# The head of a two-layer transformer kernel: pass 0's rows scaled in four copies and turned on TensorE instead of copied by DMA, and another slot table

## The reference, cut to what matters

```python
x = layernorm(x + attn0(x)); x = layernorm(x + ffn0(x))   # ffn0: int8 matmul, rounded activations
x = layernorm(x + attn1(x)); x = layernorm(x + ffn1(x))   # ffn1: silu(x Wg) * (x Wu), then Wd
# x: 4 x 1024 x 128, 16 heads of 8
def attn0(x):
    q, k, v = split(x @ qkv_w.T)                    # each 1024 x 128
    q, k = l2norm(q) / sqrt(8), l2norm(k) / sqrt(8) # norm over all 128 of a row, not per head
    return softmax(q_h @ k_h.T / temperature_h) @ v_h ... @ proj_w.T + proj_b
# attn1: per-head layernorm of q and k, rotary embedding, causal mask
```

## Time and profile before

| what | us |
|---|---|
| median of 3 runs | 812.29 (812.27 to 813.13) |
| the profiled execution | 812.69 |
| its span in the trace | 810.6 |
| PE busy | 791.2 |
| ACT busy | 767.8 |
| DVE busy | 528.8 |
| POOL busy | 174.3 |

### The profile page before, as it was taken

One profiled execution on the slowest core, in us unless ns is written; L12 is line 12 of the kernel. 1 busy time (PEld: TensorE's weight loads), 2 busy tenths in 40 slices (PEclk: granted clock), 3 DMA queues, 4 the chain that ended last, 5 costly groups with the idle time before them and its releaser, 6 DMA issues.

```text
span 810.6 us, 18434 instructions
## 1 busy us (share of the span) xinstructions
PE 791.2 (98%) x7467; PEld 295.0 (36%) x7469; DVE 528.8 (65%) x1422; ACT 767.8 (95%) x869; POOL 174.3 (22%) x370
## 2 busy tenths in 40 slices
PE   8999999999999999999999999999999999999996
...
PEclk9999999999999999999999999999999999999999
...
GB/s 148 256 230 216 122 79 81 155 41 181 144 35 156 266 40 44 179 156 80 92 208 27 128 106 43 91 128 44 91 131 51 68 131 54 27 190 110 2 28 15
DMA packets 48554, 88.71 MB, mean 109 GB/s; under 512 B 5201, under 2 KB 14545, under 8 KB 48465
## 3 DMA queue, kind: packets, MB, share of 16 engines
...
...
...
## 4 chain that ended last, share of the span: by engine, by line
PE 73%; ACT 13%; DVE 9%; issue 4%; POOL 1%; DMA 0%; ACTq 0%; DVEq 0%; POOLq 0%
PE ps L896 35%; PE ps L874 20%; ACT probs L717 13%; PE ps L763 8%; PE ps L752 3%; PE ps L849 2%; DVE th L1282 1%; DVE hT L1283 1%; PE ps L930 1%; PE ps L757 1%; DVE sums_t L1137 0%; POOL v_all L590 0%; PE ps L938 0%; PE ps L791 0%; DVE gate_sb L1279 0%
## 5 line engine op out<-in xcount | busy, mean ns | idle before, releaser
L717 ACT ACTIVATE probs<-ps 128x1024 f32<-128x1024 f32 x800 | 745.8, 1057 | 17.6 <-PE ps L874 13.8
L896 PE MATMUL ps<-probs,v_st 128*32 128x512 f32 (+3 forms) x3584 | 424.9, 556 | 3.1 <-issue 1.8
L874 PE MATMUL ps<-q_st,k_st 32*128 32x512 f32 (+3 forms) x1792 | 257.0, 458 | 3.2 <-ACT probs L717 2.3
L874 PEld LDWEIGHTS ps<-q_st,k_st 32*128 32x128 f32 x1792 | 119.4, 181 | 289.5 <-ACT probs L717 240.7
L627 POOL TENSOR_SCALAR_AFFINE_SELECT probs<-probs 128x256 f32<-128x256 f32 x256 | 103.8, 428 | 139.1 <-ACT probs L717 137.0
L896 PEld LDWEIGHTS ps<-probs,v_st 128*32 128x32 f32 x3584 | 80.1, 108 | 109.2 <-issue 80.3
L595 POOL COPY v_st<-v_all 128x256 f32<-128x256 f32 (+1 forms) x65 | 25.7, 405 | 342.1 <-PE ps L896 334.2
L1256 DVE COPY mid_qkv<-ps 128x384 f32<-128x384 f32 x32 | 17.8, 557 | 44.3 <-PE ps L763 43.8
L1137 DVE STREAM_TRANSPOSE sums_t<-ps 128x512 f32<-128x512 f32 x32 | 22.9, 717 | 26.6 <-PE ps L896 26.5
L1287 DVE TENSOR_TENSOR last_y<-ps,last_y 128x128 f32<-128x128 f32 x24 | 7.0, 292 | 42.7 <-PE ps L763 42.7
L849 PE MATMUL ps<-yTp,w_hid 128*128 128x512 f32 x84 | 30.8, 448 | 2.2 <-DVE hT L1283 0.6
(11 more groups left out here) (192 smaller groups left out, 645.2 us busy)
## 6 DMA issues: line engine op xcount, KB each, us to landing
...
q_st<-parts_scratch SPq DMA_DIRECT2D x62, 256.0 KB, 3.9
...
k_st<-parts_scratch SPq DMA_DIRECT2D x17, 256.0 KB, 2.8
xT<-in_xT SPq DMA_DIRECT2D x8, 256.0 KB, 4.4
x_all<-in_x SPq DMA_DIRECT2D x8, 256.0 KB, 6.5
out<-yo SPq DMA_DIRECT2D x7, 256.0 KB, 2.3
```

The lines of the kernel that those rows point to most:

```text
L717: nc.scalar.activation(probs[:, k % PS, :, 0:w], slot(k)[:, :, 0:w], ACT.Exp).then_inc(probs_ready, 1)
L874: last_ = mm(slot(k)[:, e, at:at + n], k_st[row, p % KB, kt * P:(kt + 1) * P], q_st[row, p % KB, lo:HALF], start=True, stop=not shifted)
L896: last_ = mm(acc[HR * h:HR * (h + 1), lo:HALF], v_st[:, p % VB, kt, h, :], probs[:, (2 * s + h // 2) % PS, h % 2, at:at + n], start=FIRST[ ...
```

## The change

The parts for pass 0 are no longer copied by DMA. DVE scales k and q of chunk 0 for the first four heads into `first_qk`, each feature four times side by side (y = 0 to 3); PE turns this, so the four copies come out on the right partitions; ACT writes the turned values times sign (1 or -1) rounded to fp32r, `first_sign`; and DVE writes turned x low + first_sign, with low 0 or 1, which is the high part for two of the copies and the negative low part for the others, to `k_st` and `q_st` in place. The second key half of pass 0 (chunk 1) is made in the same way as a new side piece, `firstT`, the first of FIRST_KEYS.

Other edits that go with it: chunk 0's projection is done as all q, all k, all v, in banks ACC, SIDE and 5; the squares of k come from DVE's batch-norm statistics, and of chunk 1 ACT takes two tiles' squares and DVE the others; the flags are worked out in two portions, the second behind the scaling; the plain scaling, turning and splitting of chunk 0 (for pass 1 and later passes) stands behind the work for pass 0, the turns behind score blocks 0 to 2; the copies for pass 1 are all issued by SP, the high part's ahead of the low part's; pass 1's second key half is copied straight from SBUF and no longer through DRAM; POOL stores chunk 1's k later in its list; SP issues the loads of later constants only when the first input is in; the zero matmuls are 8 at the start and no others. The slot table is another one throughout.

```diff
-FIRST_KEYS = [("prep", 1, "pe", "qkT", 1), ("prep", 1, "dve", "scale_q", 0), ("prep", 1, "pe", "qkT", 0)]
+FIRST_KEYS = [("prep", 1, "pe", "firstT", 1), ("prep", 1, "dve", "scale_k", 0), ("prep", 1, "pe", "qkT", 1), ("prep", 1, "dve", "scale_q", 0), ("prep", 1, "pe", "qkT", 0)]
...
-p p p - - - - <pc c <cp < p - <pp - pp |tc < <p pp
...
+- - - p pp p p <pc < pc < p - <cpp <p < |pt p < <pp
...
+    tcol, first_tcol = w_cols[:, 3 * C:3 * C + 1], w_cols[:, 3 * C + 1:3 * C + 2]
+    low_q, sign_q, low_k, sign_k = [w_cols[:, 3 * C + n:3 * C + n + 1] for n in range(2, 6)]
...
+    first_qk = job["prep"]["qkv"][:].rearrange("p t c -> p (t c)")[:, 0:TC * 2 * HR * PRODUCTS].rearrange(
+        "p (t u f y) -> p t u f y", t=TC, u=2, y=PRODUCTS)
+    first_sign = job["mid"]["part"][:, 0, :, :]
...
-    head_bank = {1: ps[:, TC, :], 0: ps[:, TC + 1, :]}
+    FIRST_BANK, V_BANK = (5, 4), 5
...
-    WARM = (10, 4, 0, 22, 7)
+    HEAD_SQUARES = 2
+    WARM = 8
...
         load_x(1)
+        sp.wait_ge(x_in[0], 16)
...
         for u, dst in ((1, k_st), (0, q_st)):
-            sp.wait_ge(parts_ready, 2 - u)
-            for y in range(PRODUCTS // 2):
-                first_rows(sp, 0, u, dst, y)
-        for u, dst in ((1, k_st), (0, q_st)):
-            for y in range(PRODUCTS):
-                first_rows(sp, 1, u, dst, y)
+            for low in range(PARTS):
+                sp.wait_ge(*((parts_ready, 2 - u) if low else (head_high, 2 - u)))
+                for y in range(PRODUCTS):
+                    if (y % PARTS if u else y // PARTS) == low:
+                        first_rows(sp, 1, u, dst, y)
         sp.wait_ge(flags_made, 1)
         far_scores = sp.value_load(far_any[0:1, 0:1], min_val=0, max_val=1)
         sp.wait_ge(side_read, FILL["prep", 1, "qkT", 1] + 1)
         for y in range(PRODUCTS):
-            sp.dma_start(k_st[y:P:PRODUCTS, 0, HALF:S].bitcast(F32),
-                         job["mid"]["part"][0:P // PRODUCTS, 1, y % PARTS, :].bitcast(F32)).then_inc(more_rows_in, 16)
+            sp.dma_start(k_st[y:P:PRODUCTS, 1, HALF:S].bitcast(F32),
+                         job["mid"]["part"][HR:2 * HR, 1, y % PARTS, :].bitcast(F32)).then_inc(second_rows_in, 16)
         store_parts("prep", 0, 1)
         store_parts("prep", 0, 0)
-        parts_sent(sp, "prep", 1, 2)
-        rows(1, 1, k_st[:, 1, HALF:S], slice(HALF, S), second_rows_in)
...
-        send_parts(pool, "prep", 1, 1)
...
-        todo = [(s + 1, 0, "mask", s) for s in range(NS) if STEPS[s][3]]
+        todo = [(slot_of("prep", 1, "qkT", 1) + 1, 0, "send", 1)] + [(s + 1, 0, "mask", s) for s in range(NS) if STEPS[s][3]]
...
+            act.wait_ge(head_qkv, 1)
             for t in range(TC):
-                act.wait_ge(head_qkv, t + 1)
-                square(0, t)
-            nc.scalar.activation(v_all[:, 0, 0, tiles_of(0), :], ps[:, 0:TC, 2 * C:3 * C], ACT.Copy).then_inc(qkv_copied, 1)
+                square(t, ps[:, ACC, t * P:(t + 1) * P], job["prep"]["st"][:, 0, 2 * t:2 * t + 1])
+            act.wait_ge(head_qkv, 3)
+            nc.scalar.activation(v_all[:, 0, 0, tiles_of(0), :], ps[:, V_BANK, :].rearrange("p (t c) -> p t c", t=TC),
+                                 ACT.Copy).then_inc(qkv_copied, 1)
             for t in range(TC):
-                if t == TC - 1:
+                act.wait_ge(head_qkv, 4 + t)
+                for u in range(2 if t < HEAD_SQUARES else 0):
+                    square(TC + 2 * t + u, ps[:, t, u * C:(u + 1) * C], job["mid"]["st"][:, 0, 2 * t + u:2 * t + u + 1])
+                if t == HEAD_SQUARES:
                     act.wait_ge(tcol_made, 1)
-                    act.wait_ge(head_turned, 2)
-                    nc.scalar.activation(job["prep"]["part"][:, 0, 0, :], head_bank[0], ACT.Copy, scale=tcol).then_inc(head_high, 1)
-                act.wait_ge(head_qkv, TC + t + 1)
-                square(1, t)
-                nc.scalar.activation(buffers("prep", 1)["qkv"][:, t, :], ps[:, TC + t, 0:3 * C], ACT.Copy).then_inc(
-                    head_copied if t < TC - 1 else qkv_copied, 1)
-            for u, dst in ((1, k_st), (0, q_st)):
-                act.wait_ge(parts_ready, 2 - u)
-                for y in range(PRODUCTS // 2, PRODUCTS):
-                    first_rows(act, 0, u, dst, y)
+                    for u in (1, 0):
+                        act.wait_ge(first_turned, 2 - u)
+                        nc.scalar.activation(first_sign[:, u, :], ps[:, FIRST_BANK[u], :], ACT.Copy,
+                                             scale=(sign_q, sign_k)[u]).then_inc(first_signed, 1)
+                op = nc.scalar.activation(job["mid"]["qkv"][:, t, :], ps[:, t, 0:3 * C], ACT.Copy)
+            op.then_inc(qkv_copied, 1)
...
+            elif what == "firstT":
+                pe.wait_ge(first_scaled, 3)
+                last_ = turn4(lambda t: first_qk[:, t, k, :, :].rearrange("p f y -> p (f y)"), side, ident)
...
-                    pe.wait_ge(rows_in[p % KB], 32 * (p // KB + 1) + (32 * PRODUCTS - 32 if p % KB < 2 else 0))
+                    pe.wait_ge(*((first_made, 2) if not p else (rows_in[p % KB], 32 * (p // KB + 1) + {0: -32, 1: 32 * PRODUCTS - 32}.get(p % KB, 0))))
...
+            if not s:
+                pe.wait_ge(parts_ready, 2)
...
-        keep_warm(WARM[0], SIDE)
+        keep_warm(WARM, 0)
         pe.wait_ge(w_in, 16)
-        for c in range(2):
-            pe.wait_ge(x_in[c], 16)
+        pe.wait_ge(x_in[0], 16)
+        for n, bank in enumerate((ACC, SIDE, V_BANK)):
             for t in range(TC):
-                mm(ps[:, c * TC + t, 0:3 * C], xT[:, c, t * P:(t + 1) * P], w_qkv[0],
-                   start=True, stop=True).then_inc(head_qkv, 1)
+                last_ = mm(ps[:, bank, t * P:(t + 1) * P], xT[:, 0, t * P:(t + 1) * P], w_qkv[0][:, n * C:(n + 1) * C],
+                           start=True, stop=True)
+            last_.then_inc(head_qkv, 1)
+        pe.wait_ge(x_in[1], 16)
+        for t in range(TC):
+            mm(ps[:, t, 0:3 * C], xT[:, 1, t * P:(t + 1) * P], w_qkv[0], start=True, stop=True).then_inc(head_qkv, 1)
         pe.wait_ge(pool_consts, 2)
+        pe.wait_ge(qkv_copied, 1)
         for u in (1, 0):
-            pe.wait_ge(head_copied, 2 - u)
-            keep_warm(WARM[2 - u], TC + 1 - u)
-            pe.wait_ge(qk_ready["prep"], 2 - u)
-            turn4(lambda t: job["prep"]["qk"][:, t, u * C:(u + 1) * C], head_bank[u], ident).then_inc(head_turned, 1)
-
-        pe.wait_ge(qkv_copied, 1)
-        keep_warm(WARM[3], 0)
-        pe.wait_ge(qkv_copied, 2)
+            pe.wait_ge(first_scaled, 2 - u)
+            for t in range(TC):
+                last_ = tp(ps[:, FIRST_BANK[u], t * P:(t + 1) * P], first_qk[:, t, u, :, :].rearrange("p f y -> p (f y)"), ident[:])
+            last_.then_inc(first_turned, 1)
+
         pe.wait_ge(flags_made, 1)
         far_scores = pe.value_load(far_any[0:1, 0:1], min_val=0, max_val=1)
+        pe.wait_ge(qkv_copied, 2)
+
+        def head_turn(u):
+
+            pe.wait_ge(qk_ready["prep"], 2 - u)
+            turn4(lambda t: job["prep"]["qk"][:, t, u * C:(u + 1) * C], ps[:, ACC + u, :], ident).then_inc(head_turned, 1)
 
         def steps(shifted):
             if shifted:
+                head_turn(1)
+                head_turn(0)
                 for name, c, e, what, k in FIRST_KEYS:
                     if e == "pe":
                         stage(name, c, what, k)
 
-            pe.wait_ge(parts_ready, 2)
             for k in range(SLOTS):
                 scores(k, shifted)
             if not shifted:
-                stage("prep", 1, "qkT", 1)
+                head_turn(1)
+                head_turn(0)
             for s in range(NS + 1):
                 for k in (2 * s + 3, 2 * s + 4):
                     if k < 2 * NS:
                         scores(k, shifted)
                     if k % 2 and s in BETWEEN:
                         sums(s - 1)
-                    if k < WARM[4]:
-                        keep_warm(2, ACC)
...
+            elif what == "firstT":
+                chain[name].link(ts(first_sign[:, k, :], side, sign_k, None, ALU.mult))
+                stt(out=k_st[:, 0, HALF:S], in0=side, scalar=low_k, in1=first_sign[:, k, :].bitcast(F32),
+                    op0=ALU.mult, op1=ALU.add).then_inc(side_read, 1)
...
+        def head():
+
+            ch, part, qk = chain["prep"], job["prep"]["part"], job["prep"]["qk"]
+            per = lambda c, k: buffers("prep", c)["st"][:, k, 0:2 * TC].rearrange("p (t u) -> p t u", u=2)
+            by_t = lambda x: x.rearrange("p (t c) -> p t c", t=TC)
+            roots = lambda c: [rows_norm("prep", c, what) for what in ("rs1", "rs2")]
+            dve.wait_ge(head_qkv, 2)
+            bn, mv, mean2 = tok["last"]["bn"], tok["last"]["st"][:, 0, :], tok["last"]["st"][:, 1, 0:TC]
+            mean, var = mv[:, 0:2 * TC:2], mv[:, 1:2 * TC:2]
+            for t in range(TC):
+                ch.step(v.bn_stats(bn[:, t, :], by_t(side)[:, t, :]))
+            ch.need()
```

(39 more changed lines are left out.)

128 lines of the change are left out of this document (59 added, 69 removed).

## The result

The changed kernel takes 821.24 us (median of 6 runs, 819.55 to 823.57), the kernel before beside it 812.55 (812.27 to 813.51, 6 runs). The ratio is 1.0104, 95% interval 1.0088 to 1.0121: slower by 1%. The forecast of 813.8 is missed by 7.4 us, and the time lies outside the range to 816.4. The six times come in two groups: 819.55 to 819.98 with a mean granted clock of 0.989 or 0.990, and 822.50 to 823.57 with 0.985 to 0.987. The profile is of an execution of 819.56 us, from the first group; its span is 817.4 us. It is compared with the profiled 812.69 of before, 6.87 less.

A forecast was written before the change was run, and what follows sets the result against it. ACT's exponentials were taken to set the pace after the head. Head -4.2, pass 1 +3.3 and the wait at block 32 +2.4 make +1.5 us: 814.2 from the profiled 812.69, 813.8 on the median's scale; range 810.2 to 816.4.

The forecast's parts named there:

- The head: Work before exponential 0: without DMA copies for pass 0 it starts at 15.4 instead of 19.61, 4.2 us sooner.
- Pass 1's rows: SP's eight copies land at 23.5, block 8 waits; exponentials 8 to 13 and slots 6 to 8 lose 3.3 us.
- The clock: PE's clock after the removed zero matmuls: taken as full, their removal worth nothing; a fall would cost 2.2 us.
- the stretch is never wholly empty: Argument against PE's clock falling between 10.5 and 23.5 us: PE has some 7 us of work in those 13.
- return of 4.4 us: After a fall, PE's clock would need 4.4 us of work to return, of which 2.2 us is lost.
- SP's chain: SP's copies, stores, then load of pass 2's rows at 45.05; q lands at 49.7, block 32 waits, +2.4 us.
- upper bound of +2.1: Exponential 33 later than before by +2.1 instead of 1.5 us, if SP's stores land 0.6 later.
- another 0.2: Side work in slots 6 to 8 costs ACT 0.2 us, part of the 3.3 us spent in pass 1.
- (c): Theory after the traces: smaller waits on DVE lie beside SP's queue, which sets when pass 2's rows land; no size.
- the rival of losses that add up: Rival after the traces: losses add up along PE, and pass 2's rows are late because all is; no chance given.
- The table: New slot table: 0, with 1.5 us to either side; as a rival it costs 1.5 us (815.3), chance 0.10.
- the clock falls: Rival: PE's clock falls in the thin stretch before block 8, adding 2.2 us for 816.0; chance 0.14.

The follow-up runs named there:

- e1_fill: The changed kernel with zero matmuls put back into PE's thin stretch, around pass 0's turns and score blocks 4 to 7; 818.82 us.
- e3: The changed kernel with zero matmuls put back in PE's thin stretch and SP's four stores of chunk 0's parts issued earlier; 813.44 us.
- e2: The changed kernel with SP's four stores of chunk 0's parts ahead of the copies that wait for `qkT` 1; 815.19 us.
- e4: The kernel before without its 26 later zero matmuls and the 2 after each of blocks 3 to 6; 814.69 us.
- e5: e3 with DVE's branch on the far-scores flag ahead of chunk 1's first units instead of behind them; 812.86 us.
- e6: e5 with chunk 2's first projection in slot 8 instead of slot 7; 811.81 us.
- e7: The kernel before with the changed kernel's slot table from slot 23 on, earlier slots as before; 812.55 us.

## Why the prediction was wrong

**The head: right.** Exponential 0 was put at 15.4 and came at 15.61. The statistics take 0.89 and 0.38 us, and the scaling in four copies costs the plain 1.29 for two, as taken:

```profile
11.25 1.29 DVE L1360 TENSOR_TENSOR prep_qkv<-ps,prep_st 128x512 f32<-128x512 f32 x2
```

**Pass 1's rows: the mechanism right.** Block 8 is released by the copies of q (23.78; predicted 23.5), exponential 8 starts at 24.61 (24.05), and exponential 13 waits because `qkT` 1 waits for DVE's scaling (the bracket at 32.40). The gap before 13 is 1.00, predicted 1.1.

**The clock: the step that failed first.** The forecast took the removed zero matmuls to be worth nothing and kept PE at full clock. "Against it: the stretch is never wholly empty" was a poor reason: the clock fell at 16.43 while PE was doing turns and score blocks, and 13.65 us passed before it rose. Its price, 2.2 us, came out (2.27 by e1_fill, 1.8 to 2.2 by e3 against e2, 1.83 in e4's trace and 2.2 by its median), but by luck: it was worked out as half of a return of 4.4 us, and the half clock lasted three times as long, while PE was busy 12.49 us in it. Some 6 us of that are loss (an estimate, half of the busy time), of which only 2.27 reached exponential 13. The chance of 0.14 was too low. What spoke for it was in the code: the kernel before multiplies zeros in just these places, and I costed their removal at nothing since they "stood in waits". With the half clock `qkT` 1 is read at 34.5 instead of the 31.4 of the forecast. Of these 3.1 us, e1_fill gives back 2.27; the rest, 0.8, is already there at full clock.

**SP's chain: the order right, two terms too small.** That a wait for pass 2's rows from DRAM would be new, and that the strict order of SP's queue makes it, was forecast, and e2_stores shows it. The sizes from the first copy on: to the last stores 7.93 us (42.44 - 34.51) against 7.5; from these to the load 8.02 against 6.14. I took the 6.14 from a trace in which chunk 0's stores lay 6 us ahead of chunk 1's; here all six follow each other without a pause, the last two issue in 2.61 us instead of 1.30, which is 1.31 of the 1.88 missed, and land in 6.2 (median) instead of 4.9 (the rows below), while the DMA share is 0.88 instead of 0.67. The upper bound of +2.1 allowed 0.6 for it, and it was 1.9. In e2, with the pause back, the same span is 6.67, of which 1.55 is issuing, and they land in 5.0. The other 0.57 stays open between the landing and SP's stand behind its branch, which end together (50.3 and 50.38); the forecast had no term for the stand, though one of up to 4.84 us may lie hidden in its 6.14. The two stores in the list of DMA issues (count, KB, median us to landing), before and then after:

```profile
parts_scratch<-mid_part SPq DMA_DIRECT2D x2, 512.0 KB, 4.9
```

```profile
parts_scratch<-mid_part SPq DMA_DIRECT2D x2, 512.0 KB, 6.2
```

The two failures make the miss: 51.7 for exponential 33, plus 3.1, 0.4 and 1.9, is 57.1; it was 57.08. On the profiled execution's scale 814.2 + 5.4 = 819.6, against 819.56. That the end fits as well is partly luck, as 0.9 us is won between exponentials 60 and 799 and 0.5 lost behind the last (the spans differ by 6.8, the shift there is 6.34). The 1.7 us from there to the median come from the three runs above 822, whose cause stays open.

**Two terms that were missed, and cost nothing here.** Slots 6 to 8 had "another 0.2". They have 1.41 (the projection in slot 7 behind DVE's read of slot 6's turn) and 0.97 (DVE's stand at the branch) on ACT. At full clock, in e3_both, exponentials 0 to 31 thus lose 6.15 us (-4.60 to +1.55), where the sum had 3.3. But exponential 33 hangs on SP's load and not on them: they made block 32 wanted later and its wait 2.47 instead of some 5. So (c) held, and the rival of losses that add up falls: the sum along ACT would count them twice. They began to cost when the clock and SP's order were repaired; e5 then won 0.7 and e6 1.4 in the trace (0.6 and 1.05 by the medians).

**The table** was given 0 with 1.5 to either side: by e7 it is between 0 and a gain of 0.9. The decline of the changed kernel's shift from 7.2 to 6.3 behind exponential 60 is nearly that of e7.

The forecast thus stood on one path, with its rival "the clock falls" costed as an addition of 2.2 to it. The range should have held the sum of that and a longer store; 816.4 did not.
